# Attention over a normalised feature map: the scores of two groups are made between the two halves of an even slot's weighing instead of ahead of the slot

## What is computed

```
xn    = groupnorm(x, 32 groups)
f, g  = Wq @ xn, Wk @ xn          # 64 x 4096 for each image
h     = Wv @ xn                   # 256 x 4096
beta  = softmax(f^T g, axis=1)    # 4096 x 4096, over the first position
out   = x + gamma * (h @ beta) + xn
```

## Time and profile before

| | |
|---|---|
| median of 3 runs | 1909.76 us (1909.17 to 1910.69) |
| the profiled execution's own time | 1909.52 us |
| its span, from the first to the last instruction | 1907.8 us |
| PE busy | 98% of the span |
| DVE, ACT, POOL busy | 86%, 82%, 69% |
| mean granted clock of the tensor engine | 0.998 |

### The profile page before, as it was taken

One profiled execution on the slowest core, in us unless ns is written; L12 is line 12 of the kernel. 1 busy time (PEld: TensorE's weight loads), 2 busy tenths in 40 slices (PEclk: granted clock), 3 DMA queues, 4 the chain that ended last, 5 costly groups with the idle time before them and its releaser, 6 DMA issues.

```text
span 1907.8 us, 44195 instructions
## 1 busy us (share of the span) xinstructions
PE 1877.8 (98%) x17369; PEld 1556.5 (82%) x17369; DVE 1642.1 (86%) x2238; ACT 1565.2 (82%) x1677; POOL 1308.9 (69%) x757
## 2 busy tenths in 40 slices
PE   6899999999999999999999999999999999999999
PEld 3688888887888888887888888888788888888888
DVE  7899999987779999997877999998887788888885
ACT  4788888987878888897877888898787788888885
POOL 4367678866656776986654766788575577767777
PEclk9999999999999999999999999999999999999999
DMA  4022112212112211211211222121130111111111
GB/s 144 4 68 71 53 33 72 59 23 63 34 30 66 76 55 24 78 53 28 65 36 40 68 56 54 51 58 46 29 72 25 23 31 33 30 28 31 32 34 35
DMA packets 200111, 91.19 MB, mean 48 GB/s; under 512 B 150240, under 2 KB 191712, under 8 KB 199904
## 3 DMA queue, kind: packets, MB, share of 16 engines
q1 hardware_dynamic: 199904, 88.36, 17.8%
HBM read 46.60 MB, written 16.78 MB: 33 GB/s over the span
## 4 chain that ended last, share of the span: by engine, by line
PE 93%; DVE 1%; issue 1%; ACT 0%; DVEq 0%
PE O L505 23%; PE O L507 23%; PE O L506 23%; PE S L493 7%; PE S L490 7%; PE S L487 6%; PE O L466 1%; PE O L465 1%; PE O L464 1%; PE O L449 1%; PE O L454 1%; PE O L450 1%; DVE SC L884 1%; ACT SC L636 0%; ACT V L653 0%
## 5 line engine op out<-in xcount | busy, mean ns | idle before, releaser
L390 POOL TENSOR_TENSOR PL<-SC,PH 128x1024 f16<-128x1024 f32 x511 | 1093.1, 2147 | 539.9 <-ACT SC L643 538.6
L505 PE MATMUL O<-V,PH 128*128 128x257 f16 x4096 | 1118.7, 273 | 1.8 <-POOL PL L418 1.7
L507 PE MATMUL O<-V,PL 128*128 128x257 f16 x4096 | 1118.5, 273 | 0.0
L506 PE MATMUL O<-V,PH 128*128 128x256 f16 x4096 | 1116.8, 273 | 0.0
L884 DVE TENSOR_TENSOR SC<-SC,MB 128x1024 f32<-128x1024 f32 x511 | 617.5, 1210 | 0.1
L642 ACT ACTIVATE PH<-SC 128x1024 f16<-128x1024 f32 x511 | 539.3, 1055 | 93.3 <-PE O L507 86.5
L636 ACT ACTIVATE SC<-S 128x1024 f32<-128x1024 f32 x512 | 504.9, 1016 | 131.8 <-issue 118.4
L841 DVE TENSOR_TENSOR XM<-S,XM 128x1024 f32<-128x1024 f32 x384 | 468.6, 1220 | 110.4 <-PE S L493 101.5
L643 ACT ACTIVATE SC<-SC 128x1024 f32<-128x1024 f32 x511 | 533.9, 1045 | 0.0
L505 PEld LDWEIGHTS O<-V,PH 128*128 128x128 f16 x4096 | 400.9, 98 | 51.3 <-POOL PL L418 2.0
L506 PEld LDWEIGHTS O<-V,PH 128*128 128x128 f16 x4096 | 400.9, 98 | 50.9
(11 more groups left out here) (117 smaller groups left out, 1073.4 us busy)
## 6 DMA issues: line engine op xcount, KB each, us to landing
xin<-x SPq DMA_DIRECT2D x24, 1024.0 KB, 5.5
xres<-x SPq DMA_DIRECT2D x64, 256.0 KB, 2.9
ATT<-OT SPq DMA_DIRECT2D x1008, 16.0 KB, 1.8
out<-RES SPq DMA_DIRECT2D x63, 256.0 KB, 2.2
SC<-x SPq DMA_DIRECT2D x8, 512.0 KB, 7.8
F<-GG SPq DMA_DIRECT2D x64, 64.0 KB, 2.0
GG<-GG SPq DMA_DIRECT2D x32, 128.0 KB, 2.4
SC<-wvT SPq DMA_DIRECT2D x1, 256.0 KB, 6.4
```

The costliest lines, as they stand in the source:

```text
L390: pool.tensor_tensor(PL[:, s % RING, :], sc(s), PH[:, s % RING, :], ALU.subtract).then_inc(pl_ready, 1)
L505: mm(o[:, 0:C + 1], PH[:, n % RING, cols], vh, start=t == 0, stop=False)
L506: mm(o[:, 0:C], PH[:, n % RING, cols], vl, start=False, stop=False)
L507: w = mm(o[:, 0:C + 1], PL[:, n % RING, cols], vh, start=False, stop=t == T - 1)
```

## The change

On the tensor engine alone, from chunk 1 on, the block of 16 score matmuls of an even slot goes from ahead of `weigh(n, 0)` to between `weigh(n, 0)` and `weigh(n, 1)`, with its own waits. In chunk 0 it stays where it was. No instruction is added or left out, and the streams of the other engines, the DMA queue's too, are what they were.

```
-            for n in range(K * G):
+            def slot_scores(n):
                 k, g = divmod(n, G)
-                b, j = divmod(k, CPB)
                 q = SCORES_AT.get(n)
                 if q is not None:
...
                     scores(q)
+
+            for n in range(K * G):
+                k, g = divmod(n, G)
+                b, j = divmod(k, CPB)
+                if k == 0:
+                    slot_scores(n)
...
                 weigh(n, 0, tiles)
+                if k > 0:
+                    slot_scores(n)
                 extra(k, g, MID)
                 if g == 0 and k > 0:
                     pe.wait_ge(osb_ready, MB2 * (k - 1) + 1)
```

## The result

| | before | after |
|---|---|---|
| median of 7 runs | 1909.63 us | 1917.02 us (1916.16 to 1917.21) |
| ratio after to before | | 1.0038, 95% interval 1.0028 to 1.0048 |
| span of the profiled execution | 1907.8 us | 1914.8 us |
| granted clock | 0.998 | 0.998 |

The kernel is 7.4 us slower. This is inside the predicted range of 1914 to 1927 us and 5 us under the predicted 1922.0 us; it is the time of the rival "the copy gets in", 1917.1 us.

The account below looks back on a forecast made before the run. PE, busy 98% of the span, was taken as bound by its own matmul stream. Terms -1.9 + 4.6 + 7.2 + 0.9 + 0.3 + 1.3 = 12.4 us on 1909.52 us gave 1922.0 us, range 1914 to 1927 us.

Parts of the forecast that it names:

- the copy gets in: Chunk 5: DVE's two-element copy beats POOL's second instruction, chunk 6 costs 3 x 0.81 us; 1917.1 us, chance 0.33.
- Term A: Start of chunk 14, three images: weighing still waits for DVE's low part, scores no longer cover it; 4.6 us lost.
- What there is to win: Four PE waits ahead of scores after chunk 0 end, covered by 12 matmuls: 1.9 us won.
- Term D: Start of chunk 62, without scores: the scaling hangs on chunk 61's last scores, 1.31 us later; 1.3 us lost.
- The ordinary starts: Second half at some 45 chunk starts waits for DVE's scaling: 0.08 us left to spare, costed at nothing.
- Term C: Slot 2 of chunks 8 to 11: POOL's low weights barely in time, 0 to 0.1 us each; 0.3 us in all.
- the first part of term B: Start of chunk 6, three images: POOL's instruction holds DVE's two-element copy, scaling comes late; 3 x 2.4 = 7.2 us lost.
- POOL's instruction depends on the same maximum through ACT's odd store: Chunk 5: store 0.84 us later, so POOL's instruction ends at 233.10, before DVE's two-element copy asks at 233.19.
- its input ready at about 232.9: Chunk 5: POOL's next instruction follows back to back, is 0.1 us old when the copy asks, may hold it 2.13 us.
- The start of chunk 7: DVE leaves a wait for POOL 0.5 us late, 0.27 us to spare before the scaling; 3 x 0.3 = 0.9 us lost.

Follow-up runs that it names:

- the reductions: Two small unused DVE reductions added in each chunk from 1 to 61: 1921.01 us in the changed kernel, 1910.43 us in the kernel before.
- one more: Changed kernel with one more unused aggregation of statistics on DVE ahead of the copy of two elements in chunk 5: 1923.43 us, ratio 1.0076.
- an undone part: Changed kernel with scores back ahead of the slot in chunks j = 5 and 6 of images 0 to 2 and slot 6 of chunk 61: 1914.75 us.

## Why the prediction was right where it was, and where not

**Right.** The change is slower, and each of its places but the start of chunk 1 was found. *Term A*: 4.6 us predicted, 4.6 in the trace, 4.5 when undone alone. *What there is to win*: 1.9 us, all four waits gone; made alone, 2.2 us. *Term D*: 1.3 us, and 1.3 measured. *The ordinary starts*: at 0.08 us to spare nothing waits; 0.07 measured with the reductions. *Term C*: 0.3 us predicted, 0.5 measured, in nine places of 0.05 us; the normalising gave the delay back as described.

**Wrong: the first part of term B**, "3 x 2.4 = 7.2 us". The trace has 3 x 0.59 = 1.8 us. The step that failed is the one in which "POOL's instruction depends on the same maximum through ACT's odd store" and the next one, "its input ready at about 232.9", follows back to back. Both exponentials between also wait for DVE's subtractions behind the maxima. The first starts 0.17 us later than the store lets it, so that the first instruction ended at 233.27 in the prediction's times and not at 233.10, behind the copy's 233.19. The second instruction's input was ready at 233.32 and not at 232.9, and it began at 233.39. This second arrow is enough alone: with the first instruction's end at 233.10 the copy would still have asked 0.2 us before the next began. The mechanism itself was right: with the copy 0.03 us late, as in the row of one more in the table, the cost is 2.77 us in each image against my 2.4 (1.45 and 1.32 in the trace), as POOL's second instruction ends 0.3 us later than I had it, and the time is 1923.4 us against my 1922.0. I chose between two outcomes 5 us apart on a margin of 0.1 us while two arrows of the chain were missing, and named the smaller one as a rival at 0.33. What is left to the 0.81 us of that rival: the copy, which waited 0.25 us before the change, no longer does, and 0.81 - 0.25 = 0.56, against 0.59.

**Mis-sized.** The start of chunk 7 had 0.3 us and measured 0.41. Chunk 1 was not in the sum: it already waited 0.13 us for the scaling, and waits 0.35, while the 0.21 us ahead of its scores are gone, so that its two halves cancel.

**Luck.** That the measured 1917.02 us meets the rival's 1917.1 is partly luck. Of the rival's terms, 2.4 us for chunk 6 was 0.6 too much, and 0.9 and 0.3 us for chunk 7 and term C were 0.5 too little.

**The sum** with the measured terms is 7.5 us for a measured 7.4.

## What to carry to other kernels

In a kernel whose bound engine has almost no waits, moving a block trades cover: list for each wait behind the moved block what there is to spare, and for each wait ahead of it what it loses, and look at both again when the move is taken back, since an undone part stood at 0.33 us of new waits. Move it only where a wait is seen: four slots of 244 gave the whole gain. Where two engines shut each other out for whole instructions, a margin of a tenth of a microsecond decides over two, so a forecast there has two values and needs every arrow of both chains, the subtractions behind the maxima too. And where a chain without a gap begins at a wait, ask what it begins at once that wait is taken away.

## What the runs showed of the hardware

A DVE copy of two elements that asked 0.03 us after a POOL instruction of 2.13 us had begun waited for the whole of it. The Trainium skill (SBUF — State Buffer, Who interferes with whom) says that whoever issues first has the shared pair of ports for the whole instruction and that the other is fully blocked. The trace agrees, with 2.13 and 1.90 us for the held copies and 0.17 for the free ones. A copy that asked 0.08 us ahead of an instruction's end lasted 0.17 us too. The 12 normalisings of the kernel before that met POOL asked 1.30 us ahead of an end and got in before POOL's next instruction (1.84 to 1.87 us instead of 0.80), which then lasted 2.58 to 2.60 us instead of 2.13. The maxima showed no such wait: all 384 of L848 lasted 1.20 to 1.23 us. Behind waits of 1.3 to 1.7 us the tensor engine's matmuls kept their distance of 0.11 us. Behind 28 of the 55 waits of 2.7 us and more, some 10 to 16 matmuls were 0.21 us apart, and the granted clock of two of the four us after one of them was 0.50, the lower level (1.2 GHz of 1.2 and 2.4). The six waits of 3.2 to 3.4 us were not among the 28, so the length alone does not decide it. In three of the changed kernel's waits the profile named a releaser (POOL's low weights) that had been done for 6.8 to 6.9 us.
